# Attention in a fused image and text block: weighted values in fewer visits, maxima of the second round in two places

## The reference, cut to what matters

```python
h = _L0_tok_ref(x, W_embed, b_embed, pos_embed)          # 64 x 196 x 256
h = jnp.concatenate([h, txt], axis=1)                    # 64 x 228 x 256
h = h + attn(layernorm(h))
h = h + ffn(layernorm(h))
# attn: 16 heads of 16, causal
scores = einsum('bhqd,bhkd->bhqk', q, k) / sqrt(16); scores[above diagonal] = -inf
ctx = einsum('bhqk,bhkd->bhqd', softmax(scores), v);  out = ctx @ Wo.T + bo
# ffn, _ternary_linear(x, w): alpha = mean(|w|); w_q = sign(w) * (|w| > alpha / 2)
#   x / rms(x) @ w_q.T, with exact gelu between the two layers
```

## Time and profile before

| what | us |
|---|---|
| median of the runs | 2009.48 |
| the profiled execution | 2009.6 |
| its span, first to last instruction | 2007.8 |
| TensorE busy | 1879.4 (94%) |
| VectorE busy | 1600.3 (80%) |
| ScalarE busy | 1326.7 (66%) |
| GpSimd busy | 733.1 (37%) |
| TensorE's granted clock, mean | 0.978 of full speed |

### The profile page before, as it was taken

One profiled execution on the slowest core, in us unless ns is written; L12 is line 12 of the kernel. 1 busy time (PEld: TensorE's weight loads), 2 busy tenths in 40 slices (PEclk: granted clock), 3 DMA queues, 4 the chain that ended last, 5 costly groups with the idle time before them and its releaser, 6 DMA issues.

```text
span 2007.8 us, 57166 instructions
## 1 busy us (share of the span) xinstructions
PE 1879.4 (94%) x24066; PEld 1561.4 (78%) x24066; DVE 1600.3 (80%) x2685; ACT 1326.7 (66%) x1922; POOL 733.1 (37%) x651
## 2 busy tenths in 40 slices
PE   5689999999999999999999999999999999999875
PEld 4678888888878888877888787888888888878654
DVE  4668888888888888888888888888888888888764
ACT  4257776676777666677667677766667776676552
POOL 1123333434333344333343434334343333434332
PEclk8789999999999999999999999999999999999987
DMA  4011121111111111111211111111111112110000
GB/s 139 24 46 29 51 55 55 51 38 45 39 50 55 53 53 37 36 48 50 55 50 54 38 32 53 50 55 50 49 38 34 52 54 56 51 38 29 17 29 24
DMA packets 66102, 93.54 MB, mean 47 GB/s; under 512 B 10082, under 2 KB 59718, under 8 KB 65592
## 3 DMA queue, kind: packets, MB, share of 16 engines
q1 hardware_dynamic: 65848, 89.90, 15.9%
HBM read 45.03 MB, written 14.94 MB: 30 GB/s over the span
## 4 chain that ended last, share of the span: by engine, by line
PE 66%; DVE 19%; issue 7%; ACT 6%; POOL 1%; DMA 0%; ACTq 0%; SPq 0%; DVEq 0%; POOLq 0%
PE dense L340 36%; PE score L340 18%; DVE gl L934 6%; PE pvps L340 5%; PE dense L397 2%; DVE rs L920 2%; DVE qm L976 2%; DVE pT_lo L910 2%; PE dense L358 2%; DVE mx L962 2%; DVE mx L961 2%; ACT sq L700 2%; ACT g L692 1%; PE dense L386 1%; ACT pT_hi L666 1%
## 5 line engine op out<-in xcount | busy, mean ns | idle before, releaser
L1174 POOL TENSOR_SCALAR_AFFINE_SELECT pr<-pr 114x1368 f32<-114x1368 f32 (+1 forms) x192 | 250.9, 1307 | 560.6 <-ACT pr L683 560.5
L683 ACT ACTIVATE pr<-score 114x1824 f32<-114x1824 f32 x192 | 325.1, 1693 | 94.7 <-PE score L340 94.3
L934 DVE TENSOR_TENSOR gl<-g 128x456 f16<-128x456 f32 x256 | 232.3, 946 | 24.4 <-ACT g L692 24.0
L340 PE MATMUL score<-qm,km 32*114 32x228 f32 (+1 forms) x4096 | 206.0, 327 | 47.5 <-DVE mx L962 43.0
L1186 POOL TENSOR_TENSOR acc<-acc,sq 128x456 f32<-128x456 f32 x192 | 239.7, 1249 | 23.2
L340 PE MATMUL dense<-wdn,g 128*114 128x256 bf16 x1024 | 238.8, 280 | 2.6 <-DVE gl L934 1.4
L340 PE MATMUL dense<-wdn,gl 128*114 128x256 bf16 x1024 | 233.2, 275 | 0.0
L340 PEld LDWEIGHTS score<-qm,km 32*114 32x114 f32 x4096 | 159.6, 177 | 83.7 <-issue 77.7
L340 PE MATMUL score<-km,qm 32*114 32x228 f32 (+1 forms) x4096 | 204.4, 325 | 6.3 <-ACT pr L683 6.1
L340 PE MATMUL pvps<-pr,vp 114*32 114x228 f32 (+1 forms) x4096 | 192.4, 317 | 12.0 <-POOL pr L1174 11.9
L920 DVE RECIPROCAL rs<-rs 128x228 f32<-128x228 f32 x128 | 200.7, 1568 | 1.7 <-DMA cxraw<-cxraw 1.7
(11 more groups left out here) (127 smaller groups left out, 4549.0 us busy)
## 6 DMA issues: line engine op xcount, KB each, us to landing
pix<-x SPq DMA_DIRECT2D x32, 588.0 KB
sq<-x SPq DMA_DIRECT2D x32, 588.0 KB
rs<-cxraw SPq DMA_DIRECT2D x256, 57.0 KB, 2.0
cxraw<-cxraw SPq DMA_DIRECT2D x256, 57.0 KB, 2.0
out<-h SPq DMA_DIRECT2D x64, 228.0 KB
h<-txt SPq DMA_DIRECT2D x32, 64.0 KB, 4.8
km<-wqkvo SPq DMA_DIRECT2D x1, 1024.0 KB, 13.7
h<-w_upT SPq DMA_DIRECT2D x1, 1024.0 KB, 14.2
```

Of the source, the lines that this page charges most:

```text
L340: return nc.tensor.matmul(*args, **kw)
L683: act(pr[q % 2][:], score[0:R, :, 0:4 * R], ACT.Exp, scale=float(HD) ** -0.5).then_inc(a["exp"], 1)
L934: tt(gl[:, m], g[:, m], hi_view(g[:, m]), ALU.subtract).then_inc(v["gl"], 1)
L1174: nc.gpsimd.affine_select(out=blocks, in_=blocks, compare_op=ALU.is_ge, fill=0.0, base=0, pattern=[[0, 4], [0, n], [1, R]], channel_multip ...
```

## The change

`VALUES` gets an empty list for group 0 of an image, and group 1 makes all four entries, two of them from the exponentials of the group before. `weighted_values` returns at once for groups 0 and 3, so a pair has four visits and not six: after rounds 0, 1, 3 and 4. All counts on the semaphore of visits become counts of four. In `maxima_unit` the two reductions can be asked for apart; in round 1 the first one now stands ahead of the low halves of pixels 3 and 4, the second where both stood. The work on ternary weights is spread anew: two absolute sums in round 4 of step 0, the third in round 1 of step 1, the product with ones in round 2, the bounds in round 3, the first piece of the down weights in round 4, the up weights in round 0 of step 2, and the last piece, as before, in round 2 of step 2.

```diff
-VALUES = [[(0, 0, 0, 2), (0, 1, 0, 1)], [(1, 0, 0, 0), (1, 1, 1, 0)],
+VALUES = [[], [(0, 0, 1, 2), (0, 1, 1, 1), (1, 0, 0, 0), (1, 1, 1, 0)],
           [(2, 0, 1, 2), (2, 1, 0, 0), (3, 0, 0, 2), (3, 1, 0, 1)]]
...
                     if isinstance(t, int) and t == 2:
-                        sp.wait_ge(v["tern"], 1)
+                        sp.wait_ge(v["tern"], 2)
...
             def weighted_values(t, u, k):
 
                 pair, q = values_of(t, k)
-                if not live(pair):
+                b, third = divmod(q, 3)
+                if not live(pair) or third == 0:
                     return
...
-                if q >= 1:
-                    eng.wait_ge(pe["pv"], count(ROUNDS, pair, q))
+                visits = (0, 0, 1, 2, 2, 3)[q]
+                if visits:
+                    eng.wait_ge(pe["pv"], count(4, pair, visits))
                 elif began(pair - 1):
-                    eng.wait_ge(pe["pv"], count(ROUNDS, pair - 1, ROUNDS))
+                    eng.wait_ge(pe["pv"], count(4, pair - 1, 4))
...
-                eng.wait_ge(pe["pv"], count(ROUNDS, pair, (2, 3, 5, 6)[k]))
+                eng.wait_ge(pe["pv"], count(4, pair, k + 1))
...
-            def maxima_unit(pair, k):
+            def maxima_unit(pair, k, parts=(0, 1)):
                 b, third = divmod(k, 3)
...
+                if 0 in parts:
+                    eng.wait_ge(pe["s"], count(ROUNDS, pair, k + 1))
...
+                    m, x = (0, 0) if third == 1 else (third // 2, 16 - 8 * third)
+                    nc.vector.tensor_reduce(mx[:, m, 1, x:128:32], score[0:R, :, 0:2 * R], AX.X, ALU.max)
+                if 1 in parts and third == 1:
                     nc.vector.tensor_reduce(mx[:, 1, 1, 16:128:32], score[0:R, :, 2 * R:4 * R], AX.X,
                                             ALU.max).then_inc(v["max"], 1)
...
                 for k in range(ROUNDS):
+                    if Bm and k == 1:
+                        maxima_unit(t - 1, k, (0,))
                     if A and k == 1:
                         pixels_lo(t, 3)
                         pixels_lo(t, 4)
...
                     if Bm:
-                        maxima_unit(t - 1, k)
+                        maxima_unit(t - 1, k, (1,) if k == 1 else (0, 1))
...
-                    if t == 1 and k in (1, 2, 3):
-                        absolute_sum(k - 1)
+                    if t == 0 and k == 4:
+                        absolute_sum(0)
+                        absolute_sum(1)
+                    if t == 1 and k == 1:
+                        absolute_sum(2)
+                    if t == 1 and k == 3:
+                        ternary_bounds()
                     if t == 1 and k == 4:
-                        ternary_bounds()
-                    if t == 1 and k == 5:
-                        ternary(0)
-                        ternary(1)
+                        ternary(1, 0)
                     if t == 2 and k == 2:
-                        ternary(2)
+                        ternary(2, 2)
...
+                    if t == 2 and k == 0:
+                        ternary(0, 1)
```

More of the change, by code:

```diff
@@ L535, in weighted_values @@
                 pair, q = values_of(t, k)
-                if not live(pair):
+                b, third = divmod(q, 3)
+                if not live(pair) or third == 0:
                     return
                 par = u if k < 5 else 1 - u
-                b, third = divmod(q, 3)
                 eng.wait_ge(p["mask"], count(ROUNDS, pair, q + 1))
-                if pair == 0 and q == 0:
+                if pair == 0 and q == 1:
                     eng.wait_ge(v["tbound"], 1)
-                if q == 0:
+                if q == 1:
                     eng.wait_ge(a["v0"], count(2, pair, 2))
@@ L549, in weighted_values @@
                     eng.wait_ge(a["raw"], count(4, pair, 2 * b + 1))
-                elif q == 3:
+                elif q == 4:
                     eng.wait_ge(a["raw"], count(4, pair, 2))
-                elif q == 0 and began(pair - 1):
+                elif began(pair - 1):
                     eng.wait_ge(a["raw"], count(4, pair - 1, 4))
@@ L593, in step @@
                         values(t - 1, 1)
-                    if t == 1 and k == 4:
+                    if t == 1 and k == 2:
                         eng.wait_ge(v["tsum"], 3)
@@ L720, in value_rows @@
                 if k == 1 and began(pair - 1):
-                    eng.wait_ge(pe["pv"], count(ROUNDS, pair - 1, 3))
+                    eng.wait_ge(pe["pv"], count(4, pair - 1, 2))
                 elif k == 0 and began(pair - 2):
-                    eng.wait_ge(pe["pv"], count(ROUNDS, pair - 2, ROUNDS))
+                    eng.wait_ge(pe["pv"], count(4, pair - 2, 4))
                 dst = vp[:, 0 if k else u + 1].rearrange("p x e c -> p (x e) c")[:, :, 0:VW:2]
@@ L893, in ternary_bounds, with ternary @@
                 eng.wait_ge(v["tbound"], 4)
-            def ternary(i):
+            def ternary(i, done):
                 up2, down2 = [z[:].rearrange("p a b -> p (a b)") for z in (wup, wdn)]
@@ L899, in ternary @@
                 ts(dst, src, tern[:, 6 + w:7 + w], None, ALU.is_lt).then_inc(v["tbelow"], 1)
-                eng.wait_ge(v["tbelow"], i + 1)
+                eng.wait_ge(v["tbelow"], done + 1)
                 nc.vector.scalar_tensor_tensor(out=dst, in0=src, scalar=tern[:, 4 + w:5 + w], in1=dst,
@@ L951, in moments @@
                     eng.bn_aggr(mv[:, j], st[:, j]).then_inc(s_mv, 1)
[L953 removed]
+            def maxima_unit(pair, k, parts=(0, 1)):
                 b, third = divmod(k, 3)
[L955 to L961 removed]
+                if 0 in parts:
+                    eng.wait_ge(pe["s"], count(ROUNDS, pair, k + 1))
+                    if k == 0 and began(pair - 1):
+                        eng.wait_ge(pe["mt"], count(2, pair - 1, 2))
+                    elif k == 3:
+                        eng.wait_ge(pe["mt"], count(2, pair, 1))
+                    m, x = (0, 0) if third == 1 else (third // 2, 16 - 8 * third)
+                    nc.vector.tensor_reduce(mx[:, m, 1, x:128:32], score[0:R, :, 0:2 * R], AX.X, ALU.max)
+                if 1 in parts and third == 1:
                     nc.vector.tensor_reduce(mx[:, 1, 1, 16:128:32], score[0:R, :, 2 * R:4 * R], AX.X,
                                             ALU.max).then_inc(v["max"], 1)
[L964 to L967 removed]
+                elif 1 in parts:
+                    nc.vector.tensor_reduce(mx[:, third // 2, 0].rearrange("p (i y d) -> p i y d", i=4, y=2)[:, :, :, 0],
                                             score[0:R, :, 2 * R:4 * R].rearrange("p i (y w) -> p i y w", y=2), AX.X,
```

13 lines of the change are left out of this document (1 added, 12 removed).

## The result

| | before | after |
|---|---|---|
| median of 4 runs, us | 2009.6 (2005.4 to 2009.8) | 1958.4 (1957.2 to 1960.3) |
| profiled execution, span, us | 2009.6, 2007.8 | 1957.2, 1955.4 |
| ratio to before | | 0.9751 [0.9734, 0.9768] |
| forecast | | 1969, range 1960 to 1992 |

The change makes the kernel 51 us faster here. On another chip it was 48.6 us (1958.3 against 2006.8).

The account below looks back on a forecast made before the run. Bound: TensorE's waits on VectorE, 1.20 us in round 1 and 0.36 before hidden_rows, in a 58.90 us step. 29 full steps x 1.20 = 34.8 us, and 6 at start and end, off 2009.6 gave 1968.8; range 1960 to 1992.

Parts of the forecast that it names:

- The wait of round 1: TensorE's wait for the columns of scores of the second reduction: to shrink from 1.20 to about 0.18 us a step.
- The product: VectorE's L923 in round 2, held by GpSimd's select: to fall from 1.05 to 0.4 or 0.5 us.
- 0.64 - 0.58 + 0.14 = 0.20: Merged visits per step: hidden_rows released 0.64 us earlier, round 3 0.58 longer, rounds 5 and 0 0.14 less.
- Together 6 us: Gain outside the full steps: 5 us at the start, the rest from the 1.58 us wait at the end losing 1.0.
- Sum 2.1 + 0.6 + 2.5 + 0.7 - 3.0 = 2.9; I add 2 for the half clock: Start: low-half wait 2.1, small sum 0.6, keys' wait 2.5, visit 0.7, step 2 -3.0; 5 us, bounds 0 and 9.
- The 3.0 lost in step 2: Start: thresholding of the up weights, 3.9 us, returns in step 2 where 0.94 us are idle: -3.0 us.
- term 2.5: Start: TensorE's wait of 2.53 us behind the keys, after thresholding in step 1, goes: 2.5 us gained.
- rival S: Product behind an accumulation, wait before hidden_rows 1.68 us, clock falls behind it each step: slower, 2029 us; chance 0.04.
- P: Rival: the product in round 2 keeps its 1.05 us; step gains 0.56 us, time 1987 us; chance 0.12.
- Q: Rival: `up` is late and gains only 0.7 us; step gains 0.9 us, time 1978 us; chance 0.12.
- R: Rival: the product in round 2 falls behind an accumulation; step gains -0.04 us, time 2004 us; chance 0.08.
- T: Rival: rows of scores are late, so the first reduction is too and round 1's wait stays; 1998 us; chance 0.04.

Follow-up runs that it names:

- after_again: The changed kernel repeated unchanged, on another chip: 1958.3 us.
- big_sum_late: The changed kernel with the absolute sum of 2048 columns in step 1 and the two of 1024 in step 0: 1963.8 us.
- maxima_only: The kernel before with only the first reduction of round 1 moved ahead: 1974.1 us.
- sum_before_select: The changed kernel with one of GpSimd's four accumulations of round 2 ahead of the select instead of behind it: 1977.5 us.
- start_only: The kernel before with only the work on the ternary weights spread anew: 2005.7 us.

## Why the forecast was too high, step by step

**Full steps: right in each term.** The wait of round 1 was to go from 1.20 to 0.18, and did (0.18 in the row). The first reduction was to cost nothing: the next low half starts where it ends. The product was to take 0.4 to 0.5: 0.42, and it ended at the select's end plus 0.25, with the margin that the prediction named. The table load has no wait, `up` isn't late. The step was to shrink by 1.20 us and shrank by 1.285: 29 x 0.085 = 2.5 us of the miss. By single edits the reduction gave 1.016 for my 1.0 and the visits 0.266 for 0.64 - 0.58 + 0.14 = 0.20; the small error is in the visits. Of what was left over, the prediction had 0.44 us before hidden_rows; it is 0.46 on the weight loads and 0.21 on the matmuls.

**Start and end: the terms that were mis-sized.** The step that failed is "Together 6 us", of which the start had 5 and the end 1. What lies outside the full steps gave 11.3 and 13.9 in two measurements, 5.3 to 7.9 more. The traces place it. The start is shorter by 9.6 us, 8.3 without step 3's own gain, where the forecast had 5; the end is shorter by 5.5, or 3.6 in after_again, where it had 1.0.

In the start, the other two edits gave what the prediction said (1.0 for the reduction and 0.7 for the visit): without the start edit 165.9 became 162.9, 1.7 without step 3's share. The edit on the ternary weights gave 6.7 for the 3.3 that remain of "Sum 2.1 + 0.6 + 2.5 + 0.7 - 3.0 = 2.9; I add 2 for the half clock". Its sums gave 3.3 for 1.1 + 0.6, of which some 1.7 are products and scores that no longer run slower behind the wait, as in big_sum_late. The 3.0 lost in step 2 were right: without that thresholding the start is 2.9 shorter. But then the old place ahead of the keys, term 2.5, was worth 3.7 + 2.9 = 6.6: the kernel with both thresholdings there is that much longer than the one with none in the way. The 2 us for the half clock had no row behind them; they were to stand for all of this and were too few. The bound of 9 for the start held.

At the end, the wait of 1.58 us lost the 1.0 of the forecast, but the groups behind it also went from 1.89, 1.78 and 1.89 us to 1.05, 1.00 and 1.05, 1.5 us by the start of `up`; step 32 shrank by 3.9 in all. The prediction had the 1.89 before it, priced it in rival S, and put it at nothing in the end.

**The base.** The sum was made against an execution of 2009.6; the medians on the other chips are 2006.8 to 2007.6. So some 2.4 us of the miss may be the base. In short, 10.4 us of miss are 2.5 for the steps and 7.9 for start and end by the first measurement; against the others' 2007.2 they are 2.5, 2.4 of base and 5.5. Some of it is luck of the execution: of the 52.4 us between the two profiled spans, 1.6 lie before the first transposes of hidden rows, where nothing was changed.

**The rivals.** P (the product keeps 1.05) and R (it falls behind an accumulation) didn't come, but maxima_only shows the first and sum_before_select the second in the flesh: at 57.88 and 58.14 us a step. Q (`up` late) didn't come: 4.89 us from the columns to `up`. T fell with the wait of round 1. S was never near, and the rise of the wait to 0.75 in sum_before_select brought no slow stretch: the granted clock is 1.00 from 300 to 1780 us there.

**Open.** By the medians the start edit gives 9 to 10 us beside the other two edits and about 2 to 3 without one of them; in the column "start" it is 6.7 against 3.3 to 5.3. So part of the difference lies where the edit changes nothing, in the first 28 us and in the last steps (start_only's end is 1.5 us longer than before's), and differs from one execution to the next. Why the rest depends on company stays open: stretches at lower clock lie in other places in each kernel, and keeping the clock up in one of them moved nothing, so this is argued and not shown. The same holds for step 32, which took both other edits to lose its slow stretch.

## What to carry to other kernels

Read a steady step from the waits and one period, term by term, and trust it to 0.1 us: here every term held within 0.1 us and they added up. Don't build the filling and emptying stages of a pipeline from the lengths of waits alone: a wait that goes can take with it a slow stretch behind it, here 1.7 us for one of 3.1 and 1.5 us for one of 1.6, which a row like 1.89 for 1.05 shows beforehand. Give them the whole range between their bounds, on the side of gain too. Size them between two fixed events of a trace, which leaves out the part that differs by chance, and by taking the edit back out of the changed kernel: the medians alone made it look like 2 or 10 us. Look at the waits of the weight loads as well as at those of the matmuls, and before moving work on one engine, see which operation of the other stands over the short one that everything waits for.

## What the hardware showed that I had not expected

- A wait on weight loads alone, 0.36 us, was worth 0.37 us a step when taken away.
- A product of VectorE that meets an operation of GpSimd ended 0.25, 0.25 and 0.26 us behind that operation's end (select before and after, accumulation in sum_before_select), even where GpSimd had the next one queued.
- The same exclusion can move by itself. The timeline of VectorE before, in round 5:

```profile
1018.41 0.63 DVE L928 TENSOR_TENSOR ct_lo<-cxraw,ct_hi 128x456 fp32r<-128x456 f32 x1 [0.74 <-ACT ct_hi L741]
1018.96 1.84 DVE L1131 TENSOR_TENSOR accl<-acc 128x456 f16<-128x456 f32 x1
```

  The select started at 1018.74 there and held `accl`; after, it started at 988.00, before `ct_lo`, and holds that: 1.64 for 0.63, with `accl` at 0.62 for 1.84. The two together take about what they took.
- One program reached the same wait, near 57 us, up to 2.6 us apart from execution to execution. In the widest pair all of it arose before 30 us, 2.1 of it in 27 products that took 0.34 us each or, 12 of them, 0.53.
- Behind a wait of 3.11 us of TensorE's the products took 0.53 us, behind one of 2.04 in the same place 0.34.
